# The low halves of the H parts on GpSimd's queue in the down stage of a gated attention and FFN block

## The reference, cut to what matters

```python
def _quant_act(x2d, reorder_index, select_num):
    g = jnp.maximum(jnp.max(jnp.abs(x2d)) / GSCALE_DIV, 1e-08)
    xr = (x2d / g)[:, reorder_index]
    n = xr.shape[1] - select_num
    normal = _fp8_block_qdq(xr[:, :n])
    outl = xr[:, n:]
    q1 = _fp8_block_qdq(outl)
    q2 = _fp8_block_qdq(outl - q1)
    return (jnp.concatenate([normal, q1, q2], axis=1), g)

h = jax.nn.silu(gate) * up              # 1024 rows x 2752 columns
Am, gm = _quant_act(h, ri_mid, SELECT)
Wd = _quant_w(w_down, ri_mid, SELECT)
y = Am @ Wd.T * gm                      # 1024 x 1024
```

## Time and profile before

| | us |
|---|---|
| median of 3 runs (845.09 to 848.07) | 846.7 |
| the profiled execution, its own time | 847.32 |
| its span, from the first to the last instruction | 845.5 |
| PE busy in the span | 744.4 (88%) |
| DVE busy | 582.8 (69%) |
| POOL busy | 344.2 (41%) |
| ACT busy | 322.3 (38%) |
| mean granted clock of PE | 0.961 of full speed |

### The profile page before, as it was taken

The page is one execution under the profiler, slowest core; times in us unless marked ns, Lnnn a source line. Parts: engine busy times, 40 slices in busy tenths (PEclk is TensorE's granted clock), DMA queues, the critical chain, the costliest instruction groups (busy, mean ns, idle before and its releaser), DMA issues.

```text
span 845.5 us, 10543 instructions
## 1 busy us (share of the span) xinstructions
PE 744.4 (88%) x3542; PEld 342.0 (40%) x3547; DVE 582.8 (69%) x980; ACT 322.3 (38%) x394; POOL 344.2 (41%) x198
## 2 busy tenths in 40 slices
PE   0589103999999999999999999999899899999998
PEld 0134002545444444444444444444543344444443
DVE  5678779994475757566666667532799999989810
ACT  3799972445152525353435344400222122212100
POOL 1535766779384848484848576600000000000000
PEclk9999655999999999999999999999999999999999
DMA  8910598339698888897989797915043476574320
GB/s 313 317 67 1 152 277 155 77 62 213 149 183 204 185 201 186 199 189 194 197 186 211 172 234 167 191 38 206 21 108 76 138 185 163 148 184 90 90 60 26
DMA packets 228245, 131.38 MB, mean 155 GB/s; under 512 B 201072, under 2 KB 212336, under 8 KB 227184
## 3 DMA queue, kind: packets, MB, share of 16 engines
q1 hardware_dynamic: 228208, 130.92, 63.5%
HBM read 61.88 MB, written 19.66 MB: 96 GB/s over the span
## 4 chain that ended last, share of the span: by engine, by line
PE 73%; DVE 9%; ACT 5%; DMA 5%; POOL 3%; issue 2%; SPq 2%; DVEq 0%; ACTq 0%
PE acc L1298 48%; PE acc L1357 24%; DMA big<-in_ctx_dram 2%; DMA mid<-wbuf 1%; POOL big L733 1%; DVE big L1581 1%; ACT big L858 1%; PE acc L1234 1%; POOL big L744 1%; POOL h_in L739 1%; ACT big L866 1%; ACT hm L895 1%; DMA wbuf<-in_L_ffn_w_up_dram 1%; DVE h_in L1867 1%; DVE h_in L1877 1%
## 5 line engine op out<-in xcount | busy, mean ns | idle before, releaser
L1298 PE MATMUL acc<-mid 128*128 128x512 f16 x1920 | 415.1, 379 | 0.0
L1298 PEld LDWEIGHTS acc<-mid 128*128 128x128 f16 x1920 | 187.8, 98 | 226.2
L1357 PE MATMUL acc<-big,mid 128*128 128x512 f16 x1056 | 232.1, 383 | 8.1 <-DMA mid<-wbuf 6.9
L1357 PEld LDWEIGHTS acc<-big,mid 128*128 128x128 f16 x1056 | 103.9, 99 | 135.7 <-issue 7.8
L823 POOL TENSOR_TENSOR h_in<-wbuf,h_in 128x1024 f16<-128x1024 f32 (+1 forms) x56 | 114.4, 2043 | 96.3 <-ACT h_in L1131 96.1
L713 POOL TENSOR_TENSOR wbuf<-wbuf,w_inv 128x1024 f32<-128x1024 f32 (+1 forms) x67 | 125.2, 1873 | 40.4 <-DVE w_inv L1488 40.4
L1604 DVE SCALAR_TENSOR_TENSOR h_out<-acc,gs,silu 128x256 f32<-128x256 f32 (+1 forms) x88 | 41.5, 472 | 120.8 <-ACT silu L967 93.3
L1482 DVE TENSOR_REDUCE tb<-wbuf 128x64 f32<-128x1024 f32 (+1 forms) x67 | 79.0, 1179 | 45.4 <-DMA wbuf<-in_L_ffn_w_gate_dram 21.2
L1131 ACT ACTIVATE h_in<-wbuf 128x1024 f16<-128x1024 f32 (+1 forms) x56 | 57.0, 1019 | 115.3 <-DVE wbuf L1494 115.3
L917 ACT ACTIVATE wbuf<-wbuf 128x1024 f32<-128x1024 f32 (+1 forms) x67 | 68.1, 1016 | 77.1 <-POOL wbuf L713 76.3
L967 ACT ACTIVATE silu<-acc,gs 128x256 f32<-128x256 f32 (+1 forms) x88 | 40.2, 457 | 71.5 <-PE acc L1298 70.9
(11 more groups left out here) (170 smaller groups left out, 597.5 us busy)
## 6 DMA issues: line engine op xcount, KB each, us to landing
h_in<-h_d SPq DMA_DIRECT2D x8, 1376.0 KB, 7.1
wbuf<-in_L_ffn_w_gate_dram SPq DMA_DIRECT2D x21, 512.0 KB, 4.5
wbuf<-in_L_ffn_w_up_dram SPq DMA_DIRECT2D x21, 512.0 KB, 4.2
h_d<-h_out SPq DMA_DIRECT2D x80, 128.0 KB, 3.4
big<-in_ctx_dram SPq DMA_DIRECT2D x16, 512.0 KB, 10.0
wbuf<-in_L_ffn_w_down_dram SPq DMA_DIRECT2D x16, 512.0 KB, 4.4
big<-in_x_dram SPq DMA_DIRECT2D x8, 512.0 KB, 6.2
x_d<-big SPq DMA_DIRECT2D x8, 512.0 KB, 5.0
```

The costliest lines, as they stand in the source:

```text
L1298: last = pe.matmul(acc[m % 4][:, 0:cols], left[:, k, s * P:(s + 1) * P], w[:, right, k, 0:cols], start=(k == 0 and left is a_hi and right ...
L1357: last = pe.matmul(acc[2 * i + hf][:], left[:, k - ks.start, :], right[:, k, hf * MW:(hf + 1) * MW], start=(k == 0 and left is hi and righ ...
```

## The change

The low halves of parts 2 to 21 are made by POOL, in the same order, by the same operation on the same operands, right behind POOL's work of the stage before. They leave DVE's queue. Parts 0 and 1, whose low halves read PSUM, stay with DVE (`lo_part`). The semaphores are the same ones.

```diff
@@ block.gpsimd, after its last unit @@
+            for n, (t, ks) in enumerate(H_PARTS):
+                if n >= PE_PARTS:
+                    pool.wait_ge(nat_h_hi, n - PE_PARTS + 1)
+                    pool.tensor_tensor(nat_part(1, ks), h_in[:, t % 2, ks.start * P:ks.stop * P], nat_part(0, ks), ALU.subtract)\
+                        .then_inc(nat_h_lo, 1)
@@ block.vector, lo_h @@
-                if n < PE_PARTS:
-                    g = n
-                    lo_part(g, g % 4, turned_part(t, 0, ks), turned_part(t, 1, ks), ks.stop - ks.start, P)
-                else:
-                    dve.wait_ge(nat_h_hi, n - PE_PARTS + 1)
-                    dve.tensor_tensor(nat_part(1, ks), h_in[:, t % 2, ks.start * P:ks.stop * P], nat_part(0, ks), ALU.subtract)\
-                        .then_inc(nat_h_lo, 1)
+                lo_part(n, n % 4, turned_part(t, 0, ks), turned_part(t, 1, ks), ks.stop - ks.start, P)
@@ block.vector, the loop over the parts @@
-                    if t >= 2:
-                        lo_h(n - 1)
...
-                elif t < 2 or ks.start > 0:
+                elif n <= PE_PARTS:
                     lo_h(n - 1)
-                else:
+                elif t >= 2 and ks.start == 0:
                     finish(t - 2, i)
                 end_part(n, i, ks)
-            lo_h(len(H_PARTS) - 1)
```

## The result

The changed kernel takes 853.0 us (median of 4 runs, 852.36 to 853.64), the kernel before, run beside it, 847.4 (845.09 to 848.27). The ratio is 1.0072, with a 95% interval of 1.0057 to 1.0087: 6.1 us slower, 4.8 to 7.4. That is the sign that was forecast, and 853.0 lies inside the range, but at its upper end: 1.5 to 2 us more than the 4.1 of the sum.

What follows compares the result with a forecast made beforehand. The end was taken as part 10's landing plus a fixed 173 us of PE work. Delays of 2.88, plus 1.19 and 0.03, make 4.1 us: 846.7 + 4.1 = 850.8 us, range 847.0 to 853.2.

Steps and rivals of the forecast that it cites:

- the sign that was forecast: Whole kernel: slower, 850.8 us against the median, 0.5% slower; chance 0.70 of being slower by over 0.3%.
- the 4.1 of the sum: Landing of part 10's DMA: 2.88 delays of DVE, 1.19 for part 10 itself and 0.03 to SP's issue, 4.1 us later.
- the near ties: Parts 4, 6, 8 and 10: POOL and DVE start almost together; POOL taken as first in part 6, DVE in the others.
- the delays up to part 9: Parts 2 to 9: DVE instructions blocked by POOL's low halves, less 0.88 saved in part 9, sum 2.88 us.
- seven of the eight small low halves lay in a gap: Parts 2 to 8: low halves stand where DVE waits for ACT's floor anyway, so removing them gives nothing; part 9's gives 0.88 us.
- no blocking: Down stage: POOL's low half runs freely beside DVE, end 0.5 us earlier, 846.2 us; chance 0.10.
- DVE keeps hold: Up to part 10: POOL gets in only where DVE stands still for ACT's floor; 2.5 us delay, 849.2; chance 0.13.
- POOL first at every near tie: Parts 4, 6, 8 and 10 all go to POOL: 5.0 us later, 851.7; chance 0.15.
- I leave that term as it is: Half clock after PE's restart at part 10, some 1.7 us, kept unchanged; a longer wait could move it about 1 us.
- 27.0 us: Tiles 2 to 7: DVE's period per tile, from 24.88 now, still below PE's 28.2, so PE stays the bound.
- the chain becomes the bound: Later tiles: if large low halves took 3.7 us, DVE and POOL's period would pass PE's; some 10 us late, 857; chance 0.04.
- the row at 23.34: Trace row where DVE started 0.01 behind POOL and lost nothing; read as showing the recorded start is not quite the claim.

Runs made afterwards that it cites:

- the dummy subtraction: Against the kernel before: DVE keeps its low halves, POOL also runs a same-shape subtraction on scratch memory nobody reads; 865.3 us in one run.

## What the prediction had right, and the step that failed

The mechanism of the prediction held, the blocking between DVE and POOL ahead of part 10's landing. The step that failed is the choice of who is first in the near ties: the delays up to part 9 were put at 2.88 us and came to 4.68. A second term was left at nothing and came to 0.93 us, the half clock behind the longer wait. That 853.0 still lies in the range owes to the rival that had the ties right.

**Right: where the bound is.** The end is the landing of part 10 plus a fixed piece of PE work. The restart at part 10 moved by +5.05, +4.69, +0.42 and +3.62 us in four kernels, the runs, by their ratios, by +6.1, +4.7, +0.4 and +2.9, and what the change took from DVE in each later tile was worth nothing. Only where part 10 is made early does part 11 take over. **Right: seven of the eight small low halves lay in a gap.** Taking them from DVE gave nothing; only part 9's was in the open.

**Right: the blocking, in both directions, and its sizes.** Where the prediction had the right engine first, the delays came as worked out: part 3 0.09, part 6 1.14, part 7 0.47, each as forecast, and parts 2 and 9 0.07 and 0.04 for 0.09 each. POOL's undisturbed times were 1.16, 0.91, 1.40, 1.64 and 2.85 for 1.15, 0.90, 1.39, 1.64 and 2.87. The rivals "no blocking" and "DVE keeps hold" are ruled out by the long rows of L1875 (1.26 for 0.33 in part 5).

**Wrong: "Parts 4, 8 and 10 are at 0.08, 0.06 and 0.08, nearer to the first, so DVE is first".** POOL was first in all three. Measured: part 4 0.94 for 0.24, part 8 1.20 for 0.17, part 10 itself 0.38 for 1.22 with SP (an error the other way, since POOL first delays DVE there and not its own DMA). Part 5 was taken to be POOL's, but behind L1867 and not ahead of it, and cost 0.73 for 0.59. The delays up to part 9 add up to 4.68 in place of 2.88, and with part 10 to 5.06: the rival "POOL first at every near tie", priced at 5.0, to a tenth. I had given it 0.15. The reason was one row, where a DVE instruction that started 0.01 behind POOL lost nothing. Why it lost nothing no run shows; it has four columns, and POOL's instruction there is not the form of the low half. It says that a tie of 0.01 can go to DVE, but nothing of 0.05 to 0.08, by which POOL was ahead in parts 4, 8 and 10; the rule beside it, that whichever starts first gets hold, gave POOL all three. The prediction asked how near each tie was to a row in time, and not whether the row was of the same kind.

**Wrong: "I leave that term as it is".** The half clock behind the third wait costs more when the wait is long. Windows of after (busy by engine, granted clock, DMA share, GB/s), against the earlier trace rows:

```profile
672.00:674.60 2.60, 0.00 (x0) 0.00 (x0) 2.56 (x2) 0.00 (x0) 0.00 (x0) 0.50 1.07 186
...
678.00:680.00 2.00, 2.00 (x6) 0.73 (x5) 1.79 (x8) 0.27 (x1) 0.00 (x0) 0.50 0.00 0
680.00:682.00 2.00, 2.00 (x10) 0.88 (x9) 1.96 (x2) 1.11 (x1) 0.81 (x1) 1.00 0.00 0
```

The clock is at 0.50 already during the wait, and stays there until about 680, 5.3 us behind PE's restart; in before it fell 1.2 us behind the restart and stayed for 3.3. That is the 0.93 us in the 792 matmuls. Waits of 2.8 to 3.9 us gave 172.8 us in four executions (of three kernels), and waits of 7.2 to 7.6 gave 173.5 to 174.0 in four (of three). The text had "about 1 us either way" for it; the sum should have had it as a term, since the same sum made the wait more than twice as long.

**Wrong, without a cost: "27.0 us" as the tile's period.** POOL was first at L1869 in every tile as well, 0.07 ahead, so that step lost 2.64 instead of 1.11 (and the one at the tile's start 2.66 for 2.56): the period is 28.6 us (POOL's low halves of parts 12 and 14 start at 695.09 and 723.73). PE needs 28.5 for its 132 matmuls at full clock (156.87 / 726 x 132), where the prediction had 28.2, so the chain of DVE and POOL was already the slower one. PE still did not wait, since each tile loses only 0.1 us: POOL's last low half starts at 824.3, needs 2.85 and then 5.2 for its DMA, 832.4, and PE wants it 14.3 us ahead of its end at 848.4, at 834.1. Of a slack of some 2 us at part 11, 1.7 were left. So the rival "the chain becomes the bound", at 0.04, was nearer than its chance said: some 0.4 us more per tile would have used the slack up, and the dummy subtraction shows what comes then.

Sum by what was measured: 847.3 + 5.1 + 0.9 = 853.3 against the profiled execution, and 846.7 + 6.0 = 852.7 against the median of the three runs that I had; the runs give 853.0.

## What to carry to other kernels

Before work moves from VectorE to GpSimd, look where its instructions stand: one that fills a gap in which VectorE waits anyway is free there, and on GpSimd it blocks every VectorE instruction beside it that has two SBUF inputs or a fast form. Work the delays out one by one; where GpSimd starts first even by 0.05 us it is first, and for closer ties work out both cases. And where one landing sets the end, the order on the queue ahead of it is worth more than the queue's load: moving three steps and making one early gave 4.6 us, where taking twenty instructions off the engine lost 6.

## What was not expected of the hardware

- In a near tie recorded starts do not decide: GpSimd won from 0.01 to 0.05 us behind, and VectorE once from 0.02 us ahead and once from 0.01 behind (the row at 23.34).
- A memset on GpSimd delays VectorE's one-input fast form (0.56 became 1.50) and leaves instructions with two SBUF inputs alone (0.69 stayed 0.69).
- PE's granted clock falls to 0.53 in part 0 in some executions of one kernel and not in others, for 1.2 to 1.3 us of the time of DVE's chain. That is a fifth of the 6.1 us to be measured here, so single executions had to be compared stretch by stretch.
- Ahead of parts 10 and 11, behind waits of 1.60 and 1.79 us PE kept its full clock; behind 2.8 to 3.9 us it lost it for a short stretch, behind 7.5 us for a longer one.
